# Matmuls of ones by ones into an unread bank, placed in TensorE's pauses

## The reference

```python
x = x + tanh(g_xattn[0]) * causal_conv_mixer(ctx, ctx, layernorm(x))      # "ln 0", stage L0 xattn
x = x + tanh(g_ffn[0])   * moe_32_experts_top4_plus_shared(layernorm(x))  # "ln 1", L0 ffn
x = x + tanh(g_xattn[1]) * quantised_attention_16_heads(layernorm(x))     # "ln 2", L1 xattn
x = x + tanh(g_ffn[1])   * moe_16_experts_top2_plus_shared(layernorm(x))  # "ln 3", L1 ffn
x = x + tanh(g_xattn[2]) * attention_with_projections(layernorm(x))       # "ln 4", L2 xattn
x = x + tanh(g_ffn[2])   * ternary_gated_mlp(layernorm(x))                # "ln 5", L2 ffn
x = x + tanh(g_xattn[3]) * masked_attention(layernorm(x), ctx)            # "ln 6", L3 xattn
x = x + tanh(g_ffn[3])   * moe_8_experts_top2_capacity(layernorm(x))      # "ln 7", L3 ffn
```

## Time and profile before

| | us |
|---|---|
| median of 3 runs | 884.41 |
| lowest and highest | 879.35, 884.89 |
| the profiled execution | 886.11 |
| its span, first to last instruction | 884.4 |

### The profile page before, as it was taken

How to read it: one execution, slowest core, us unless ns; L and a number is a source line. 1 busy time by engine, 2 the same in 40 slices (tenths; PEclk the granted TensorE clock), 3 DMA queues, 4 the chain that set the end, 5 groups by cost and what they waited for, 6 DMA issues and landing times.

```text
span 884.4 us, 14478 instructions
## 1 busy us (share of the span) xinstructions
PE 703.4 (80%) x5311; PEld 497.6 (56%) x5356; DVE 534.9 (60%) x1248; ACT 373.0 (42%) x670; POOL 304.4 (34%) x332
## 2 busy tenths in 40 slices
PE   4996798998687778786889971982966479999997
PEld 3434465667355555555647850471445447777776
DVE  4796855658999999996485546737876520000014
ACT  4002122335999999996312323342753122222110
POOL 3751140000377777775017415300320071000024
PEclk9997899999698998987989995896988579999999
DMA  7311074620399999999304847000022132514414
GB/s 235 137 61 48 17 159 149 209 74 1 44 185 173 176 179 181 180 178 174 105 8 134 147 146 239 10 0 1 1 86 105 49 96 83 208 59 173 161 39 119
DMA packets 139133, 100.08 MB, mean 113 GB/s; under 512 B 109204, under 2 KB 125238, under 8 KB 137016
## 3 DMA queue, kind: packets, MB, share of 16 engines
q1 hardware_dynamic: 132552, 81.19, 38.5%
q0 software_dynamic: 6224, 17.96, 7.7%
q10 hardware_dynamic: 288, 0.00, 0.0%
HBM read 61.15 MB, written 10.72 MB: 81 GB/s over the span
## 4 chain that ended last, share of the span: by engine, by line
PE 46%; DVE 22%; issue 18%; ACT 6%; POOL 4%; DMA 4%; POOLq 0%; DVEq 0%; SPq 0%; ACTq 0%
PE psum L2389 7%; PE psum L2408 6%; PE psum L1708 3%; PE psum L879 3%; DVE xnT L1486 3%; DVE both L329 2%; PE psum L214 2%; DVE both L333 2%; PE psum L635 2%; ACT both L1377 2%; PE psum L1278 2%; PE psum L1985 2%; DVE stats L142 2%; POOL both L568 2%; PE psum L1723 2%
## 5 line engine op out<-in xcount | busy, mean ns | idle before, releaser
L1153 POOL TENSOR_SCALAR both<-both 128x1024 f16<-128x1024 f32 x128 | 133.7, 1044 | 157.2 <-ACT both L1377 151.6
L1486 DVE TENSOR_SCALAR_CACHE_REDUCE xnT<-psum,both 128x1024 bf16<-128x1024 f32 x128 | 157.4, 1277 | 10.1 <-PE psum L1278 9.9
L1377 ACT ACTIVATE both<-psum,both 128x1024 f32<-128x1024 f32 x128 | 153.8, 1208 | 9.2 <-DVE xnT L1486 8.4
L1278 PE MATMUL psum<-both 128*128 128x512 bf16 x215 | 76.7, 426 | 40.7 <-ACT both L1377 37.7
L2389 PE MATMUL psum<-both 128*128 128x320 f32 x256 | 73.8, 442 | 3.8 <-ACT both L556 3.8
L1299 PEld LDWEIGHTS psum<-both 128*128 128x128 f16 x1024 | 63.7, 98 | 20.2 <-DMA both<-both 5.8
L2468 ACT ACTIVATE both<-psum 128x320 f32<-128x320 f32 x64 | 27.7, 437 | 110.3 <-PE psum L2389 92.4
L1299 PE MATMUL psum<-both 128*128 128x16 f16 x1024 | 68.2, 171 | 3.6 <-DMA both<-both 1.7
L1300 PE MATMUL psum<-both,minus_base 128*128 128x16 f16 x1024 | 66.8, 170 | 0.0
L1300 PEld LDWEIGHTS psum<-both,minus_base 128*128 128x128 f16 x1024 | 59.0, 98 | 12.1 <-issue 4.0
L2389 PEld LDWEIGHTS psum<-both 128*128 128x128 f32 x256 | 48.9, 194 | 24.2 <-issue 5.5
(11 more groups left out here) (382 smaller groups left out, 1456.3 us busy)
## 6 DMA issues: line engine op xcount, KB each, us to landing
both<-in_l_experts SPq DMA_DIRECT2D x50, 384.0 KB, 3.7
both<-in_l_experts SPq DMA_DIRECT2D x16, 1024.0 KB, 5.5
grouped_y_dram<-both SPq DMA_DIRECT2D x31, 128.0 KB
ctok<-in_ctx SPq DMA_DIRECT2D x2, 1024.0 KB, 7.6
both<-kpad_dram SPq DMA_DIRECT2D x1, 2048.0 KB, 8.0
moe_xn_dram<-xn POOLq DMA_DIRECT2D x4, 512.0 KB, 3.9
both<-bp SPq DMA_DIRECT2D x2, 1024.0 KB, 12.3
moe_y_dram<-both POOLq DMA_DIRECT2D x7, 256.0 KB, 2.9
```

The costliest lines, as they stand in the source:

```text
L1153: nc.gpsimd.tensor_scalar(r2[n % RSLOTS2], e2[:, n % ESLOTS2, :], 255.0, HALF_BASE, ALU.mult, ALU.add).then_inc(sem("r2_ready"), 1)
L1278: last = nc.tensor.matmul(bank[2 * (n % SRING2) + half], qz2[:, h % 2, h // 2, t * P:(t + 1) * P], kT2[:, h // 2, half * 512:(half + 1) * ...
L1377: nc.scalar.activation(e2[:, n % ESLOTS2, :], scores_at(n), ACT.Exp, bias=bias2[:, n:n + 1], scale=s2[:, t * H2 + h:t * H2 + h + 1], accum ...
L1486: nc.vector.tensor_scalar(scaled2[n % 2], scores_at(n), ns2[:, t * H2 + h:t * H2 + h + 1], None, ALU.mult, ALU.min, accum_out=bias2[:, n:n ...
```

## The change

`keep_busy(i, n)` issues `n` matmuls of `onesb` by `onesb` repeated four times (128 x 512, bf16) into `bank[i]`, with no semaphore. 162 of them are put into TensorE's program at 20 places; the count of 0 in the ternary loop issues nothing. `tokens_tensor` gets a hook ahead of its second half. No other instruction is changed, added or moved.

```diff
+        def keep_busy(i, n):
+            for _ in range(n):
+                nc.tensor.matmul(bank[i][:], onesb[:], bcast(onesb[:], 1, 4), start=True, stop=True)
-            def tokens_tensor(self, pe):
+            def tokens_tensor(self, pe, between=None):
                 n = 0
                 for t in range(NT):
+                    if t == 4 and between:
+                        between()
# l0f_tensor
             shared0.up_tensor(pe, 1)
-            moe0.tokens_tensor(pe)
+            keep_busy(7, 7)
+            moe0.tokens_tensor(pe, lambda: keep_busy(7, 6))
+            keep_busy(7, 2)
             moe0.wait(pe, "token_ready", 2)
             shared0.down_tensor(pe, 0)
# l1x_tensor
                 if n >= LAG2:
                     values(n - LAG2)
+                if n - LAG2 >= U - 3:
+                    keep_busy(5, (6, 2, 2)[n - LAG2 - (U - 3)])
             pe.wait_ge(sem("o2_ready"), H2 // GH2)
# l1f_tensor
             shared3.up_tensor(pe, 1)
+            keep_busy(4, 5)
             moe3.tokens_tensor(pe)
+            keep_busy(4, 3)
             moe3.wait(pe, "token_ready", 1)
             shared3.down_tensor(pe, 0)
             shared3.down_tensor(pe, 1)
+            keep_busy(0, 5)
             pe.wait_ge(sem("map3_ready"), 1)
# l2x_tensor
-            ln_tensor(pe, 4)
+            keep_busy(5, 24)
+            ln_tensor(pe, 4, lambda: keep_busy(5, 11))
# l2f_tensor
                 if t < NT:
                     up(t)
+                else:
+                    keep_busy(4 + t % 2, (8, 7, 0)[t - NT])
                 if 2 <= t < NT + 2:
                     turn(t - 2)
# l3x_tensor
-            ln_tensor(pe, 6)
+            keep_busy(4, 3)
+            ln_tensor(pe, 6, lambda: keep_busy(4, 9))
             pe.wait_ge(sem("ctx_loaded"), 32)
             attn6.tensor(pe, 20)
+            keep_busy(7, 21)
# l3f_tensor
             router_tensor(pe, E7, rw7, bank[4], 7)
+            keep_busy(7, 11)
             moe7.positions_tensor(pe, bank[5])
+            keep_busy(7, 13)
             moe7.tokens_tensor(pe)
+            keep_busy(7, 5)
             pe.wait_ge(moe7.sem("diag_ready"), 1)
             pe.wait_ge(sem("small_consts"), 6)
             for half in range(2):
                 nc.tensor.matmul(bank[6 + half], ...).then_inc(sem("codes7_done"), 1)
+            keep_busy(4, 12)
             moe7.turn_rows_tensor(pe, 0, 0, bank[2], 0)
```

## The result

| | us |
|---|---|
| changed kernel, median of 6 runs | 877.06 (872.03 to 881.10) |
| kernel before, median of 6 runs beside them | 884.65 (879.35 to 889.59) |
| ratio | 0.9897, 95% interval 0.9866 to 0.9928 |
| profiled execution of the changed kernel, its span | 881.10, 879.4 (before 886.11, 884.4) |

So -7.6 by the medians and -5.0 by the two profiled executions, where 11.2 less was forecast: right direction, inside the range, about two thirds of the size.

A forecast was written before the change was run, and what follows sets the result against it. TensorE's matmuls, 46% of the chain, were taken to run at half clock after pauses. Terms summed to -11.2 us: 886.1 to 874.9, less 1.7 for the median of runs, 873.2; forecast's own range 868 to 877, widened to 866 to 880.

The forecast's parts named there:

- rival 1: Clock does not last from ones to work; router, ln 4, last layer's start lose 5.2 us: 878.4; chance 0.20.
- Rival 2: Transposes do not hold the clock; ln 7's transposes and router stay slow, 3.4 us lost: 876.6; chance 0.05.
- The root: Whole kernel: the ones raise the mean granted clock above 0.892; otherwise the prediction is wrong at its root.
- rival 3: Matmuls of ones do not raise the clock and outlast their pauses: +13.6 us, 898; chance 0.05.
- L2 xattn: Ones ahead of ln 4 and between its halves speed transposes and first projections: -2.8 us, range -2.0 to -2.95.
- L0 ffn: Down products at full clock, -1.85, but the last gather's landing at 130.9 bounds the gain: -1.2 us, 0.8 to 1.85.
- L1 xattn's end: Ones around units 125 to 127 delay work, transposes return part: net +1.2 us, range 0 to +2.9.
- L1 ffn: Gain of over 1.5 us ahead of the blocks becomes a new wait at block 4: -0.4, range 0 to -1.
- Ternary end: Ones in two pauses ahead of L2152; both groups of eight transposes gain some 0.35 each: -0.7 us.
- L3 xattn: Ones in three pauses ahead of L214; transposes and attention's first scores at full clock: -1.5 us.
- L3 ffn's rest: 41 ones after the router; row transposes and last layer's first products faster: -2.4 us, range -1 to -2.75.
- ln 7 and its router: L3 ffn, behind 21 ones: transposes -0.8, router -2.6; sum -3.4 us, range -1 to -4.1.

The follow-up runs named there:

- e10_ring_short: Changed kernel without L1 xattn's ones, more ones at attention 3, ln 7 and L3 ffn's tokens, 32 products of 128 columns at the experts' pause; 0.9864, 873.35 us.
- e1_late_places: Changed kernel without the 38 ones of its first three places (L0 ffn, L1 xattn's end, L1 ffn); ratio 0.9887 to the kernel before.

## Why the prediction was partly right

**The time.** 877.06 lies at the high end of the forecast's own 868 to 877, nearer to rival 1's 878.4 than to 873.2. It is above the 875.6 below which the prediction said "faster" (chance 0.71); by that line it is "same" (chance 0.25), though the ratio's interval stays clear of 1. The number alone does not choose between forecast and rivals 1 and 2, the traces do. The low end was added up wrongly: the best case of -14.7 off 884.4 is 869.7, not 868.

**The root held.** Ones raise the clock, the chain runs through TensorE at most places, and rival 3 is out: of the 24 ones ahead of ln 4 nine ran slow (12 were assumed), of all 162 some 36, and only at L1 xattn and at L2 xattn's eleven did ones hold real work back.

**L0 ffn:** -1.79, at the good end of the range, in ten profiles of ten. The step that failed is the bound by the last gather: it was issued at 119.9 again, but landed after 9.9 us instead of the 11.1 of the earlier trace rows, and the transposes began at 130.00 instead of 131.71. A landing read once is no fixed time. The gathers' landings and the transposes:

```profile
DMA to landing us min/median/max: 3.4/4.1/9.9
...
130.00 0.92 PE L556 MATMUL psum<-ident,both 128*128 128x128 f32 x6 [0.30 <-ACT both L563]
```

**L1 xattn's end:** a loss, as forecast, 0.9 against 1.2: VectorE's L1502 came 1.98 late, and 1.11 came back at the transposes, which ran at the full clock. The group by line, PE, 415.5 to 426 us, against 3.4 us for the same 16 in the earlier trace rows:

```profile
L214 PE MATMUL psum<-ident,xn 128*128 128x128 f32 x16 | 2.0, 276 | 0.4 <-DVE xn L1513 0.4
```

**L1 ffn:** the new wait is there. The chain in order of time:

```profile
473.77 3.84 DMA both<-grouped_xn_dram,grouped_token_of
477.61 0.04 issue
477.65 0.44 PE psum L1713 x2
```

3.3 us gained ahead of the blocks, 3.0 lost at block 4, whose transposes begin 0.87 later than in the earlier trace rows. But the gain ahead of the blocks came in three kernels without ones too; against those this place is worth over a microsecond in some profiles and nothing in others. What tells them apart is the clock in the first blocks, here in the changed kernel and in `e10_ring_short`:

```profile
472.00:482.00 10.00, 7.21 (x41) 1.00 0.44 120
...
472.00:482.00 10.00, 8.09 (x37) 0.83 0.53 144
```

It held in the five profiles with ones that stand at -0.30 to -0.44, and fell in the three others with ones (+1.05 to +1.60) and in all five without. So the ones made this place better in some executions only; eight profiles against five do not settle by how much.

**L2 xattn:** -2.10 where the clock fell once more during the eleven ones, so that eight of them ran at 0.43 each and held the second half back; -3.3 in eight other profiles, more than the forecast, since a fall in the attention behind it was gone as well. Those eight lost 0.8 to 1.2 again at the ternary layer's start, but so did two kernels without ones at L2 xattn.

**Ternary end:** the number was right and its cause unproven: both kernels without ones there gained the same 0.78 against the first profile of before. The hit is luck.

**L3 xattn and L3 ffn's rest:** -1.54 and -2.82 against -1.5 and -2.4. The first is the same in ten profiles of ten; the second went down to -1.30 where the clock fell again.

**ln 7 and its router** are the step that failed in the profiled execution, and rival 1 had the mechanism: the clock didn't last from the ones to the work. The prediction had counted ones against three pauses together (7.2 of 9.6 us) and took the remainder as small; it was 3.4, and 1.9 of it lay in one piece ahead of ln 7. With 21 ones the clock held twice and fell once, a mean of -2.6; with 30 it held in six profiles of six. Rival 2 is out as it was put: in those the 16 transposes ran at 1.00 and the router behind them began at 1.00. Whether transposes and router hold the clock for longer is not shown: in four of the six it fell again during the router's last one to six products, with TensorE never idle. The Trainium skill, TensorE: Matmul & The Clock Gate, section "Part 4: PE-mode transpose", says that transposes do not count as busy in the same way and the full clock does not engage; that 16 of them ran at 1.00 in 2.47 us disagrees with the second half, and says nothing on the first.

**What the sum lacked:** +1.8 at the experts' pause and +1.2 to +1.8 at the last store. For the first, the list of low stretches came from one execution of before, in which the clock happened to hold there, which was luck; it fell in six of nine profiles without ones at that pause, with and without L0's. For the second, the prediction took the 162 ones as costing nothing but TensorE's time, and not as instructions that can shift where the program is fetched.

## What to carry to other kernels

Fill a pause to its end, up to the instruction that the next engine releases: in one execution a remainder of 1.9 us undid 4.7 us of ones, while 16 small products in a wait for weights brought up to 1.8 us. Before pricing low-clock stretches, take a second profile of the same kernel; places that are low in both are worth a term of the sum, the others a fraction of one. And when instructions are added to one engine, see in the trace whether an instruction fetch now falls on a DMA issue that other engines wait for.

## What the runs showed of the hardware that was not expected

- The same program's granted clock fell at other places in other executions: at the experts' first pairs in one of two profiles of the kernel before, at ln 7's router in one of two of the changed kernel (6.83 against 3.85 us).
- TensorE can look busy and lose the clock: between 669.8 and 673.5 us no pause was longer than 0.18 us, and L1936 started at 0.50.
- A 16 KB instruction fetch and a slow DMA issue on SyncE (1.1 to 1.9 instead of 0.32 or 0.45 to 0.50 us) stood together in all eight profiles in which the fetch fell at L1 ffn's last store or the two issues behind it, and neither in the others. In all eight the slow issue ended 0.35 to 0.40 us after the fetch did. A fetch beside an issue is not enough, though: earlier stores that met one took 0.32 (`before` at 497.70, `e1_late_places` at 515.86 us). The Trainium skill, Runtime: NRT & Kernel Launch, section "Instruction fetch mechanics", calls the cost of crossing into the next 16 KB block mostly hidden; here it was a microsecond on the path once it met the last store. Why the issue is slow there stays open, and so does whose instructions the fetch brings: that its place moved when instructions of TensorE were added is all that the runs show.
